# A decoder layer on one core: the bias of the four-head norms formed by VectorE, and the normalisation moved to the head of the next step

## The reference, cut to what matters

```python
def _ln(x, w, b):
    mu = jnp.mean(x, axis=-1, keepdims=True)
    var = jnp.mean(jnp.square(x - mu), axis=-1, keepdims=True)
    return (x - mu) * jax.lax.rsqrt(var + EPS) * w + b
...
q = _fp8_linear_pertensor(ln_out, wq, wq_scale, q_in_scale).reshape(b, s, g, hpg, d)
q = _ln(q, qln_w, qln_b)
k = _fp8_linear_pertensor(ln_out, wk, wk_scale, k_in_scale).reshape(b, s, g, d)
k = _ln(k, kln_w, kln_b)
v = _fp8_linear_pertensor(ln_out, wv, wv_scale, v_in_scale).reshape(b, s, g, d)
core = _gqa(q, k, v).reshape(b, s, nh * d)
...
```

## Time and profile before

| | |
|---|---|
| median of 3 runs | 1264.98 us (1264.97 to 1266.2) |
| the profiled execution, its own time | 1269.58 us |
| its span in the profile | 1267.8 us, 19453 instructions |
| PE busy | 1196.8 us, 94% |
| DVE busy | 947.8 us, 75%, 2826 instructions |
| ACT busy | 811.6 us, 64%, 2325 instructions |
| POOL busy | 608.8 us, 48%, 722 instructions |
| the chain that ended last | PE 51%, DVE 26%, ACT 16%, POOL 4% |

### The profile page before, as it was taken

The page is one execution under the profiler, slowest core; times in us unless marked ns, Lnnn a source line. Parts: engine busy times, 40 slices in busy tenths (PEclk is TensorE's granted clock), DMA queues, the critical chain, the costliest instruction groups (busy, mean ns, idle before and its releaser), DMA issues.

```text
span 1267.8 us, 19453 instructions
## 1 busy us (share of the span) xinstructions
PE 1196.8 (94%) x6408; PEld 818.9 (65%) x6432; DVE 947.8 (75%) x2826; ACT 811.6 (64%) x2325; POOL 608.8 (48%) x722
## 2 busy tenths in 40 slices
PE   4999989789999999999999999999999998999998
PEld 2676666556677666676666777676677765555545
DVE  4669988999888887799999966657777877463341
ACT  4566558767877875676667765566787676652230
POOL 1728774654453454555555732124454534363370
PEclk9999889899999999999999999999999999899999
DMA  8211100012110221113233221041112100000000
GB/s 265 81 50 36 33 1 1 1 34 60 58 51 18 63 80 58 54 63 104 87 108 98 60 79 38 17 141 58 46 30 58 48 28 1 1 1 11 20 1 29
DMA packets 25461, 65.61 MB, mean 52 GB/s; under 512 B 2720, under 2 KB 8992, under 8 KB 25360
## 3 DMA queue, kind: packets, MB, share of 16 engines
q1 hardware_dynamic: 25088, 64.00, 16.4%
q10 hardware_dynamic: 272, 0.36, 0.1%
HBM read 59.37 MB, written 4.98 MB: 51 GB/s over the span
## 4 chain that ended last, share of the span: by engine, by line
PE 51%; DVE 26%; ACT 16%; POOL 4%; issue 2%; DMA 1%; SPq 0%; ACTq 0%; POOLq 0%
PE ps L869 10%; PE ps L1133 8%; PE ps L1066 7%; ACT big L799 5%; PE ps L859 5%; PE ps L1182 4%; PE ps L1028 3%; PE ps L961 3%; DVE big L412 3%; DVE big L981 2%; ACT big L964 2%; PE ps L993 2%; PE ps L500 2%; DVE big L654 2%; DVE big L240 2%
## 5 line engine op out<-in xcount | busy, mean ns | idle before, releaser
L869 PE MATMUL ps<-big 128*125 128x512 bf16 x1152 | 265.7, 380 | 0.1
L799 ACT ACTIVATE big<-ps,big 112x128 f32<-112x128 f32 (+1 forms) x512 | 192.4, 456 | 72.0 <-POOL big L429 69.6
L869 PEld LDWEIGHTS ps<-big 128*125 128x125 bf16 x1152 | 156.0, 137 | 80.7 <-issue 1.0
L428 POOL TENSOR_TENSOR big<-big 112x4 f32<-112x4 f32 (+1 forms) x128 | 39.2, 306 | 320.9 <-ACT big L423 320.8
L859 PE MATMUL ps<-big 128*112 128x512 bf16 x768 | 186.9, 387 | 5.2 <-ACT big L889 1.3
L658 POOL TENSOR_TENSOR big<-big 128x448 f32<-128x448 bf16 x96 | 103.6, 1080 | 110.2 <-DVE big L978 69.1
L859 PEld LDWEIGHTS ps<-big 128*112 128x112 bf16 x768 | 100.0, 132 | 68.6 <-issue 6.1
L981 DVE TENSOR_SCALAR big<-big 112x112 f32<-112x112 f32 (+1 forms) x256 | 132.7, 539 | 6.8
L412 DVE BATCH_NORM_STATS2 big<-ps 112x6 f32<-112x128 f32 (+1 forms) x512 | 113.3, 283 | 21.5 <-PE ps L869 19.4
L964 ACT ACTIVATE big<-ps,big 112x375 f32<-112x375 f32 x128 | 74.6, 583 | 83.9 <-DVE big L963 82.8
L1028 PE MATMUL ps<-big 125*128 125x224 f32 (+1 forms) x512 | 122.5, 362 | 4.2 <-DVE big L1010 3.4
(11 more groups left out here) (117 smaller groups left out, 2353.3 us busy)
## 6 DMA issues: line engine op xcount, KB each, us to landing
big<-in_ctx_t SPq DMA_DIRECT2D x32, 375.0 KB, 3.4
big<-in_w_s SPq DMA_DIRECT2D x16, 512.0 KB, 3.6
big<-in_w_p SPq DMA_DIRECT2D x16, 512.0 KB, 3.7
big<-in_w_x SPq DMA_DIRECT2D x16, 512.0 KB, 3.8
big<-in_w_g SPq DMA_DIRECT2D x16, 512.0 KB, 3.8
big<-in_w_d SPq DMA_DIRECT2D x8, 512.0 KB, 4.2
big<-in_w_a SPq DMA_DIRECT2D x8, 384.0 KB, 5.1
scr<-big SPq DMA_DIRECT2D x24, 128.0 KB, 1.7
```

The source lines that it names most:

```text
L799: t = act(lambda e, j=j: e.activation(z[0:rows, 128 * j:128 * j + 128], bk[0:rows, 128 * j:128 * j + 128], ACT.Identity, bias=rr[0:rows, 4 ...
L869: t = pe(lambda e, k=k, s=s, u=u, n=n: e.matmul(bk[0:CK, :], cT[:, s, k, CK * c:CK * c + CK], w[:, u, k, col:col + 512], start=n == 0, sto ...
```

## The change

`ln_rstd` no longer issues the two POOL operations for a four-head norm. The bias is formed by one VectorE operation, (mean * -1) * r, in a new step `p_q` that has lag 2 and stands at the head of the tick. `p_z` moves from lag 1, late in the tick, to lag 2, right behind `p_q`. One-head norms (ScalarE alone) are as they were.

```diff
@@ ln_rstd
-            tq = pool(lambda e: e.tensor_tensor(s["q"], s["mean"], r, ALU.mult), t)
-            s["tr"] = [t, pool(lambda e: e.tensor_scalar(s["q"], s["q"], -1.0, None, ALU.mult), tq)]
-            return s["i"], s["rr"], s["tr"]
+            s["te"] = t
+            return s["i"], s["rr"], None
@@ p_rstd
                 si, rr, tr = ln_rstd(it["st"])
-                it.update(si=si, rr=rr, tr=tr)
+                it.update(si=si, rr=rr)
+
+        def p_q(it):
+            if it["what"] != "v":
+                s = it["st"]
+                it["tr"] = [s["te"], dve(lambda e: e.scalar_tensor_tensor(
+                    s["q"], s["mean"], -1.0, s["r"], ALU.mult, ALU.mult), s["te"])]
@@ order
-        order = [("p", 1, p_stats), ("p", 1, p_vhi), ("a", 3, t_s2), ("a", 0, t_s0), ("p", 1, p_rstd), ("a", 5, t_s4),
-                 ("p", 3, p_t), ("b", 6, b_4), ("b", 3, b_2), ("a", 1, t_s1), ("p", 1, p_z), ("a", 8, t_s6),
+        order = [("p", 2, p_q), ("p", 2, p_z), ("p", 1, p_stats), ("p", 1, p_vhi), ("a", 3, t_s2), ("a", 0, t_s0), ("p", 1, p_rstd), ("a", 5, t_s4),
+                 ("p", 3, p_t), ("b", 6, b_4), ("b", 3, b_2), ("a", 1, t_s1), ("a", 8, t_s6),
                  ("a", 4, t_s3), ("p", 0, p_mm), ("b", 2, b_m), ("b", 4, b_3), ("b", 1, b_1), ("b", 0, b_0)]
```

## The result

The changed kernel takes 1338.7 us (1331.97 to 1339.77, 4 runs) against 1265.59 us (1264.97 to 1268.6, 4 runs): a ratio of 1.0554, with a 95% interval of 1.0526 to 1.0581. It is slower, as forecast, but by 73 us and not 35, outside the range given. The profiled execution took 1339.34 us.

A forecast was written before the change was run, and what follows sets the result against it. PE was taken as the limit, with VectorE close behind in X0 and limiting S0's first 80 us. Terms 23 + 5 + 5 + 3 = +36 us on the profiled 1269.58, 1301 by the median, gave 1300 us; range 1264 to 1318.

The forecast's parts named there:

- The mechanism: POOL's large operations start sooner and hold L981 (+0.91 us ternary, +0.79 quantization ticks) and the new operation (0.8 us each).
- The added work per X0 batch: X0 with ternary units: 0.8 new operations, 2.6 L981 and 3.2 new operations held, together 6.6 us on VectorE.
- less 2.84 idle: X0 with ternary units: VectorE's 2.84 us idle per batch is given back in full, leaving 3.8 of 6.6 us.
- the bank is released later, but no PE operation takes it sooner than a tick after: Normalisation's PSUM bank: its later release stops no PE operation; nothing entered in the sum.
- rival 4: The bank kept longer stops PE, every item's L859 or L869 finding none free: 1290 us, chance 0.02.
- The term for X0: X0 with ternary units, six batches at 3.8 us each: +23 us, bounds -4 and +51.
- S: S0's first 80 us +5 us (bounds -10 and +14), the rest of S +5 us (bounds 0 and +15).
- my -2 us: S0's first 80 us: the shorter ScalarE to POOL to ScalarE link gains 2 us, bounds 0 and -10.
- rival 1: Faster, the shorter link wins: at most -10 us in S and -4 in X0, 1256 us, chance 0.10.
- X1: X1 with ternary units, six batches: 8.3 us idle covers the 7 added, save 0.5 a batch: +3 us.
- Rival 3: VectorE full throughout X0 and S: +6 us per X0 batch, +1.5 in S and X1; 1334 us, chance 0.10.
- The signs in the profile: L797 0.4 us or more, L986 about 0.7, VectorE up 50 or more, X0 batch 41 to 42, PE waiting for VectorE.

The follow-up runs named there:

- e13: Changed kernel with the bias made by ScalarE, plus the new VectorE operation at the tick's head, result unused and not waited for: 1330.37 us, 1.0501.
- e14: e9 with one wait more: the normalisation also waits for the added VectorE operation, its bias still from POOL's pair: 1289.6 us, 1.0181.
- e6: Changed kernel with the bias operation and the normalisation behind the next item's statistics instead of ahead of them: 1301.32 us, 1.028.
- e1: Kernel before with only the normalisation moved to the head of the next tick; POOL's pair still makes the bias: 1260.2 us, 0.9959.
- e5: Kernel before with only the scaling step moved ahead of the quantization and the ternary unit: 1258.62 us, 0.9941.
- e9: e1 with the new VectorE operation added at the head of the tick, its result unused; POOL's pair still makes the bias: 1279.43 us, 1.0103.
- e4: Changed kernel with the scaling step (reciprocal and L986) moved ahead of the quantization and the ternary unit: 1292.31 us, 1.0204.
- e3: Changed kernel with the bias made by four one-number VectorE operations, one tensor input each, instead of one with two tensor inputs: 1326.35 us, 1.0472.
- e8: Changed kernel with the bias operation on VectorE but the normalisation in its old place, late in the tick of the root: 1357.49 us, 1.0727.

## Why the prediction was wrong in size

- *The mechanism* was right as far as it went: POOL's large operations start sooner and hold the scaling, and the new operation is held. The added work per X0 batch was right too: I had 6.6 us more on VectorE, and the batch from 590.8 to 637.9 has 41.74 us busy against 35.16, which is 6.58. That it agrees so closely is luck. Three of five L797 are held there and not four (3.5 us in place of 4.0), and one L368 is held instead, +0.7 us, of which I had nothing.

```profile
590.80:637.90 47.10, 41.80 (x193) 27.26 (x193) 41.74 (x112) 27.45 (x69) 17.98 (x14) 0.93 0.23 72
```

- *The first step that failed is "less 2.84 idle".* One later batch of the kernel before, of e13 and of the changed kernel:

```profile
614.70:652.70 38.00, 37.64 (x191) 26.20 (x192) 35.13 (x106) 26.66 (x69) 21.31 (x25) 1.00 0.30 91
```

```profile
644.50:688.10 43.60, 39.42 (x191) 25.73 (x192) 41.47 (x111) 31.65 (x94) 18.10 (x15) 1.00 0.26 78
```

```profile
637.20:684.70 47.50, 42.21 (x194) 27.48 (x194) 41.80 (x111) 27.37 (x69) 17.97 (x14) 0.93 0.24 72
```

  e13 has both holdings and no late bias. VectorE has 6.3 us more work there and the batch is 5.6 us longer; its idle time goes from 2.9 to 2.1 us. So 0.7 us came back and not 2.84. The two largest pieces of the 2.9 us are waits for ScalarE, not room behind PE:

```profile
616.18 1.79 DVE L240 TENSOR_TENSOR big<-big 128x750 bf16<-128x750 f32 x2 [0.76 <-ACT big L239]
...
628.10 0.29 DVE L366 TENSOR_SCALAR big<-big 128x512 bf16<-128x512 bf16 x1 [1.04 <-ACT big L356]
```

  The first stays as it is. The second goes, as I said, but the new operation brings a wait of its own, which I had named and not entered in the sum for X0:

```profile
656.94 0.16 DVE L801 SCALAR_TENSOR_TENSOR big<-big 112x4 f32<-112x4 f32 x1 [0.43 <-ACT big L423]
```

- *The second step that failed, and the larger one in X0, is "the bank is released later, but no PE operation takes it sooner than a tick after"*, which I put at nothing in the sum and gave 0.02 as rival 4. The sentence is so, and doesn't help. Going through the takes and releases of the pool in the order of the program, for a ternary X0 batch: before, the banks of its five norms went, late in the next tick, to `b_m` (three), and two ticks later to `t_s0` and `t_s2` (one each). After, all five go to `t_s0` (two) and `t_s2` (three) near the head of the next tick. The trace agrees: PE's waits for L804 in X0 are before L966 (`t_s0`) and L998 (`t_s2`). With the bias out of VectorE's queue, which is behind in just those ticks, PE stands for it. e14 prices that at 2.8 us a batch, 3.9 by the changed kernel against e13 (47.5 - 43.6 above, ScalarE's extra work in e13 aside). So the 9.5 us of a later batch are 5.6 for work and holding and 3.9 for the late bias.
- *Most of the 3.9 us is PE's clock.* PE is busy 42.21 us in the changed kernel's batch, 39.42 in e13's: 2.8 us for the same matmuls, at a granted clock of 0.93 against 1.00. e6 shows the same by itself. In three later batches PE has the same two waits for L804 (0.2 and 2.9 us), and only the clock differs:

```profile
585.80:627.20 41.40, 38.19 (x192) 26.42 (x194) 38.74 (x111) 25.72 (x68) 18.11 (x14) 1.00 0.24 74
627.20:670.30 43.10, 39.88 (x192) 27.19 (x193) 39.45 (x111) 27.42 (x70) 17.96 (x14) 0.96 0.29 89
670.30:714.50 44.20, 40.99 (x192) 27.88 (x193) 38.87 (x111) 27.34 (x69) 17.96 (x14) 0.92 0.26 77
```

  A clock of 0.92 in place of 1.00 costs 2.8 us a batch there, 0.96 costs 1.7.
- *The term for X0*, +23 us for six batches, measured: from the 16th sum to that at 729.2 us +43.9 for five of them, and +4.9 before.
- *S*: forecast +10, measured -2 at its 12th sum and +5 at its 16th, where ternary ticks already run. e1 is 12 us ahead of before by the 16th sum, and against e1 the changed kernel lost 539.4 - 522.4 = 17 us. So there was a gain as well as a loss. Whose gain it is stays open: e1 keeps POOL's pair, and e5, which leaves the normalisation where it was, is 10 us ahead there as well. It doesn't show that the shorter link, my -2 us and rival 1's -10, was worth so much.
- *X1*, +3, measured 68.1 - 52.0 = +16, of it 10.5 in the four batches from 875.7 to 1025.8. Of some 7 us of work a batch (VectorE's busy time rose by 6.9), its idle time of 8.3 us covered only 4.3, by the same error. In e9 and e4, with one holding each, the same four batches take what they took before; in e13, with both, 1.4 us more each, and in the changed kernel 2.6. The rest came in the last three batches.
- *Rival 3* named 1334 us, near the measured time, but by other parts: +6 in each X0 batch (9.2 measured), +1.5 in each of S (none in most), +1.5 in X1 (2.6). That it comes out near is luck. Its chance of 0.10 was too low for the first reason above: it was the one case that gave no idle time back.
- *The signs in the profile*: seen were L797 at 0.6 us, L986 at 0.72, L369 waiting for the reciprocal alone, VectorE up by more than 50 us. Two were not. The batch of 41 to 42 us in place of 38.00 takes 47.1 to 47.6. And PE's waits are not mainly for VectorE (3.9 us before L1033 for L1015, 3.8 before L998 for L986) but for ScalarE's L804, 24.2 us before L966 alone.
- *In the sums*, the upper bound of the X0 term, "8.5 us more" and +51, doesn't follow from its parts: 6.6 + 4 x 0.35 = 8.0 us a batch give +48.
- *The rule on engine selection* in the Trainium skill, GPSIMD Engine Reference, section 4.1 Engine selection, gives elementwise work on a tile to VectorE; followed here alone it would have let one expect a faster kernel. The bare price agrees (148 ns at the least against 0.31 us), and the kernel is 5.5% slower: the rule prices the operation, not the queue that it joins.
- *The held operation*: the Trainium skill, SBUF — State Buffer, Who interferes with whom, says that a VectorE operation with at most one SBUF input, outside the two-port modes, doesn't contend with GpSimd (POOL). e3's operations behave so, 216 ns at the most in 512; no run shows which mode they ran in.

Not settled: where the gain in S comes from, and why e8 is so much worse. No run was made for either.

## What to carry to other kernels

Before small operations are taken off an engine's queue, ask what stood behind them and what that will collide with: here two small POOL operations kept larger ones out of VectorE's way. Added work on an in-order engine may be set against its idle time only wait by wait: ask what each wait ends on, and whether that moves. Where a buffer is given back later, follow it to the next operation that takes it. And a value on which a PSUM bank's release depends should come from an engine that is ahead, not from the one that is behind: waiting for the cheap operation on the late engine cost 2.8 us a batch (e14 against e9), and PE's clock was part of that price.

## What the runs showed of the hardware

A VectorE operation of four numbers per row with two SBUF inputs is held by a large POOL operation until that one ends: 63 of 128 L797 took 986 to 1122 ns and ended 17 to 25 ns after POOL's, the others 148 to 165 ns. But a tensor_scalar of one number with its factor from SBUF never was (193 to 216 ns in 512, 278 of them inside a large POOL operation). The first I expected; that the second is free of it although L981, also a tensor_scalar, is held (1366 ns at the most before) I did not. PE was busy 0.75 of the 4 us from 622 to 626 us, and its clock was at 0.50 in the next 4; twelve matmuls of 512 columns took 4.16 us there in place of 2.75. Not each such wait is followed by the lower clock: in e6 a wait of 2.90 us at 618.85 was not, one of 2.89 us at 703.26 was.
